# A gated cross-attention and mixture-of-experts kernel: VectorE's order in the second expert stage

## The reference, cut to what matters

```python
def _L1_ffn_ref(x, Wg, W1, b1, W2, b2, W3, b3):
    weights, indices = _gate(x2, Wg)            # 4 of 16 experts per token
    for e in range(E):
        we = jnp.sum(weights * (indices == e), axis=-1)
        h = jax.nn.silu(x2 @ W1[e].T + b1[e]) * (x2 @ W3[e].T + b3[e])
        y = y + (h @ W2[e].T + b2[e]) * we[:, None]
```

## Time and profile before

| | |
|---|---|
| median of 3 runs | 2151.57 us (2151.31 to 2154.27) |
| the profiled execution | 2151.75 us |
| its span, first to last instruction | 2150.0 us |
| PE matmul busy | 1955.2 us (91% of the span) |
| DVE busy | 1348.4 us (63%) |
| POOL busy | 1147.7 us (53%) |
| ACT busy | 917.3 us (43%) |

### The profile page before, as it was taken

One profiled execution on the slowest core, in us unless ns is written; L12 is line 12 of the kernel. 1 busy time (PEld: TensorE's weight loads), 2 busy tenths in 40 slices (PEclk: granted clock), 3 DMA queues, 4 the chain that ended last, 5 costly groups with the idle time before them and its releaser, 6 DMA issues. The chain is left out here.

```text
span 2150.0 us, 40169 instructions
## 1 busy us (share of the span) xinstructions
PE 1955.2 (91%) x11418; PEld 1350.0 (63%) x11418; DVE 1348.4 (63%) x4050; ACT 917.3 (43%) x2321; POOL 1147.7 (53%) x1375
## 2 busy tenths in 40 slices
PE   5999999999999279999769999999999559999997
PEld 4777777777777168888635555555555425555554
DVE  3677777777776533223248888878888525555554
ACT  2434344444433323333247767766766213333332
POOL 1344444444444345454437888888888514444444
PEclk8999999999999689999979999999999579999999
DMA  6011101011116023333211111111117364555554
GB/s 167 26 39 27 39 27 39 27 39 37 29 53 229 8 40 52 53 50 55 43 33 36 54 54 55 55 50 50 55 55 228 99 189 81 82 82 82 80 84 64
DMA packets 140296, 142.25 MB, mean 66 GB/s; under 512 B 31626, under 2 KB 130674, under 8 KB 139832
## 3 DMA queue, kind: packets, MB, share of 16 engines
q1 hardware_dynamic: 94282, 86.60, 13.9%
q0 software_dynamic: 37888, 44.51, 12.9%
q10 hardware_dynamic: 7918, 8.57, 1.2%
HBM read 89.88 MB, written 51.94 MB: 66 GB/s over the span
## 5 line engine op out<-in xcount | busy, mean ns | idle before, releaser
L779 POOL TENSOR_SCALAR prob<-prob,rc 100x363 f32<-100x363 f32 x256 | 157.1, 623 | 355.3 <-DVE rc L634 355.3
L1826 POOL DMA_INDIRECT out<-y,xr x115 | 177.9, 1547 | 246.9 <-DVE y L1857 131.6
L1924 PE MATMUL psG<-expert_w,xgT 128*128 x460 | 219.6, 600 | 2.7 <-ACT xgT L1885 2.7
L980 PE MATMUL psJ<-wkv,cTn 96*121 96x512 f32 x384 | 180.8, 609 | 0.0
L558 ACT ACTIVATE prob<-psS,nm 100x361 f32<-100x361 f32 x256 | 141.6, 561 | 53.9 <-DVE nm L629 50.6
L1525 POOL DMA_INDIRECT acc<-y,slots x57 | 90.3, 1584 | 136.5 <-DVE y L1619 129.4
L629 DVE TENSOR_REDUCE nm<-psS 100x2 f32<-100x722 f32 x128 | 115.1, 899 | 71.8 <-PE psS L457 71.6
L1432 POOL DMA_INDIRECT rows<-row,pos_of x128 | 137.8, 1077 | 35.6 <-issue 30.1
L1889 ACT ACTIVATE gate<-pre 128x256 f32<-128x256 f32 x115 | 47.9, 416 | 249.6 <-DVE pre L1842 249.6
L1941 PE MATMUL psD<-expert_w,hT 128*128 x460 | 128.9, 402 | 12.6 <-ACT hT L1895 8.1
L1596 DVE TENSOR_TENSOR hid<-psU,gate 128x512 f32<-128x512 f32 x57 | 39.4, 692 | 159.1 <-PE psU L1716 159.1
(11 more groups left out here) (307 smaller groups left out, 5100.2 us busy)
## 6 DMA issues: line engine op xcount, KB each, us to landing
xr<-rows SPq DMA_DIRECT2D x115, 136.5 KB, 2.6
expert_w<-in_L_ffn_moe_w SPq DMA_DIRECT2D x8, 1024.0 KB, 13.8
bias<-in_L_ffn_b ACTq DMA_DIRECT2D x3, 2048.0 KB, 15.9
ctx<-in_ctx SPq DMA_DIRECT2D x32, 181.5 KB
cT<-in_ctxT SPq DMA_DIRECT2D x32, 180.5 KB
cT<-in_ctxT SPq DMA_DIRECT2D x64, 90.2 KB
expert_w<-in_L_ffn_moe_w SPq DMA_DIRECT2D x8, 512.0 KB, 12.7
expert_w<-in_L_ffn_W1T SPq DMA_DIRECT2D x16, 256.0 KB
```

The lines of the kernel that those rows point to most:

```text
L779: g.tensor_scalar(prob[:, q, :], prob[:, q, :], rc[:, q:q + 1], 1.0, ALU.mult, ALU.mult).then_inc(prob_done, 1)
L980: mm = t.matmul(ph[0:rows, 0:cols], lhs, wt[:, k, :], start=k == 0, stop=k == 1)
L1826: g.indirect_dma_start(acc, bass.IndirectOffsetOnAxis(row_token[:, j % RING, :], 0), y[:, j % 4, :], None, compute_op=ALU.add).then_inc(sc ...
L1924: mm = t.matmul(psG[:, r, :], xT[:, r, k, :], w13[:, bass.ds(e, 1), k, :], start=k == 0, stop=k == 1)
```

## The change

The step `hidden` is cut in two. `biased(j, e)` is the bias addition that writes `pre`, and `hidden(j)` is the multiplication that writes `hid`. In round j, DVE now does `biased(j+1)`, then reads the expert of tile j+2, then `weighted(j-2)`, then `hidden(j+1)`. `biased(j)` also waits for the gate of tile j-2, which reads the buffer that it writes. The registers with the expert's number are kept in a list from `biased` to `weighted`, so that each number is read once. PE, ACT, POOL and SP have the same instructions in the same order.

```diff
+                def biased(j, e):
+                    v.wait_ge(g_mm, j + 1)
+                    if j >= 2:
+                        v.wait_ge(g_out, j - 1)
+                    v.tensor_tensor(pre[:, j % 2, :], psG[:, j % 2, :], bias[:, bass.ds(e, 1), 0:2, :].rearrange("p e k f -> p (e k f)"),
+                                    ALU.add).then_inc(pre_done, 1)
+
                 def hidden(j):
-                    r, e = j % 2, expert(j)
-                    v.wait_ge(g_mm, j + 1)
-                    v.tensor_tensor(pre[:, r, :], psG[:, r, :], bias[:, bass.ds(e, 1), 0:2, :].rearrange("p e k f -> p (e k f)"),
-                                    ALU.add).then_inc(pre_done, 1)
                     v.wait_ge(g_out, j + 1)
                     if j >= 2:
                         v.wait_ge(h_mm, j - 1)
-                    v.tensor_tensor(hid[:, r, :], pre[:, r, F:2 * F], gate[:, r, :], ALU.mult).then_inc(hid_done, 1)
-
-                def weighted(j):
-                    e = expert(j)
+                    v.tensor_tensor(hid[:, j % 2, :], pre[:, j % 2, F:2 * F], gate[:, j % 2, :], ALU.mult).then_inc(hid_done, 1)
+
+                def weighted(j, e):
...
+                e_of = [expert(j) for j in range(2)]
                 v.wait_ge(bias_in, 16 * 3)
+                biased(0, e_of[0])
                 hidden(0)
                 for j in range(NT):
+                    if j + 1 < NT:
+                        biased(j + 1, e_of[j + 1])
+                    if j + 2 < NT:
+                        e_of.append(expert(j + 2))
                     if j >= 2:
-                        weighted(j - 2)
+                        weighted(j - 2, e_of[j - 2])
                     if j + 1 < NT:
                         hidden(j + 1)
-                weighted(NT - 2)
-                weighted(NT - 1)
+                weighted(NT - 2, e_of[NT - 2])
+                weighted(NT - 1, e_of[NT - 1])
```

## The result

The changed kernel takes 2112.26 us in the median of 4 runs (2109.79 to 2118.66), the kernel before 2151.72 us (2151.31 to 2154.27). The ratio is 0.9821, with a 95% interval of 0.9804 to 0.9838: 39 us less. The profiled execution took 2113.48 us, its span is 2111.7 us.

What follows compares the result with a forecast made beforehand. VectorE's closed round of 3.37 us a tile was taken as the bound, against PE's 3.022. Gains of 36.9 and 2 us less 6 for row buffers make 32.9: 2151.75 - 32.9 = 2118.9, so 2119 us, range 2110 to 2132.

Steps and rivals of the forecast that it cites:

- VectorE's ring: In the last expert stage, VectorE's closed round of dependent steps and waits: 3.37 us a tile, busy for 1.90 us of it.
- PE's own pace of 3.022 us: Time per tile where PE is not held, read from five row transposes at the start of the last stage.
- The first term: Steady part of the last stage: 106 tiles at 3.022 us in place of 3.370, 36.9 us less.
- VectorE's new round: VectorE's steps per tile after the change, from one `pre` to the next possible one: 2.46 us.
- The ring of row buffers: Load of tile j+8 waits for scatter of tile j; late scatters at 15 boundaries cost 0.4 us each, 6 us.
- The end: After the last row transpose, the last `pre` and the steps behind it come sooner: 2 us less.
- the front: Start of the stage, where VectorE waits for the bias loads: nothing moves there.
- Rival B: `y` and `hid` each hold POOL's scatter once, 0.8 us on its path; boundaries cost 15 us: 2128 us, chance 0.03.
- rows 13: POOL's scatter instructions: 1542 to 1682 ns in all 115 cases, 1546 in the middle, never held for the length of `hid`.
- Rivals A: Row buffers hold PE more often as landings get slower: 18 us in place of 6, 2131 us, chance 0.14.
- C: VectorE keeps the pace with a round of 3.2 us: 18 us gained and 1 at the end, 2133 us, chance 0.05.
- D: `hid` comes too late, so PE waits with its hidden transpose in every tile: 11 us slower, 2162 us, chance 0.02.

## Why the prediction was right, and where it was off

- The bound was VectorE's ring and not PE: right, and each of three ways to shorten it gave PE's pace. But the sum of 201.2 busy and 155.5 idle us, 3.365 a tile, proves nothing, though I used it as proof: busy and idle of any engine add up to the stretch. In the changed kernel, where PE is the bound, VectorE's 199.2 busy and 136.4 idle us make 335.6 of 334.9 as well. What told was who ended the idle pieces: reads ("issue"), the gate and its own `yb`, and never PE.
- PE's own pace of 3.022 us, read from five tiles at the start, held for 106: right to the third digit. The first term of 36.9 us came as 34.8, and the missing 2.1 are the ring's waits.
- VectorE's new round: I had 2.46 us, it is 1.95. I had put 0.15 us between steps that don't depend on each other; they overlap instead. It changed nothing here, but the same error made me miss the kernel with one uncovered read.
- The ring of row buffers: the mechanism was right, the term was mis-sized, and this is the step that failed: "I take 0.4 us for each of the 15: 6 us". It is 2.1 us in all, 0.14 each. What there was to spare came out nearly as worked out: `y` ends 14.1 us after its tile's transpose, as I had it, and the load is issued 4.5 us before use in the middle (5.95 before). But I took the size of a typical boundary from two of the longer ones, 5.55 and 6.84 us; the 16 distances over 4.2 us between two scatters were 5.3 on average before. In the changed kernel the long distances between two scatters (16 of them over 4.2 us) are 4.5 to 6.2 us, 5.0 on average, 2.0 more than a round: just what there is to spare. The one of 6.84 us did not come back.
- The end: 2 us forecast, 2.5 measured.
- Forecast 2119, measured 2112.26: of the 6.6 us, 4 are the ring, 0.5 the end, and 1 the front, where kernels and runs differ by that much without cause in this stage; the profiled run lies 1.2 above the median. The result is 0.4 us below what I had for a PE that is never held (2112.7).
- Rival B, that steps of VectorE hold up the scatters in every tile, did not come. But my reading of rows 13, that this trace does not agree with the rule, was wrong. The Trainium skill ("SBUF — State Buffer", section "Who interferes with whom") says that a VectorE step with two SBUF inputs contends with a GpSimd instruction that reads SBUF. The longest scatter before, 1.68 us, is such a case, and so is the longest of the changed kernel, 1.74 us: `hid` had just started when they started.

```profile
1947.87 0.43 DVE L1847 TENSOR_TENSOR hid<-pre,gate 128x256 f32<-128x256 f32 x1 [0.48 <-ACT gate L1889]
1948.03 1.68 POOL L1826 DMA_INDIRECT out<-y,xr  x1 [0.30 <-issue]
```
```profile
2010.46 0.42 DVE L1850 TENSOR_TENSOR hid<-pre,gate 128x256 f32<-128x256 f32 x1
2010.55 1.74 POOL L1826 DMA_INDIRECT out<-y,xr  x1 [3.39 <-DVE y L1859]
```

  A `hid` that starts later within a scatter costs it nothing: 90 of them lie wholly inside one before, and these scatters took 1.54 to 1.57 us. So the price is at most 0.27 us (1.81, the longest with the extra additions, for 1.546), and few scatters pay it.
- Rivals A, C and D did not come. What the prediction left out is that removing the read would alone have been enough. I counted the reads (0.36 and 0.48) and the gate (0.48) in the ring and treated them as one edit, though 3.37 - 3.02 = 0.35 is no more than the smallest of them, so that each was enough by its own size.

Open: why 7 buffers cost 3.57 us a tile and not 3.3 with boundaries on top (40 us forecast, 56 measured in the steady part). The lower clock makes 3.6 of the 16 us that are missing, and where the trace has the landing, loads took 2.8 us on average, where I had counted 2.3; the rest was not looked into.

## What to carry to other kernels

When an engine is busy for 97% by the profile, look at the distance between starts in a stretch where nothing holds it, and compare it with the steady distance: here 3.02 and 3.37 us. Then look at the idle pieces of the suspected partner and at what ended each of them. If none was ended by the busy engine, the partner is the bound, and only the shortfall (0.35 us) has to be removed, by whichever edit is simplest, and no more. A read into registers belongs behind a step that another wait follows, and it should be done once.

A wait at the start of a stage can cost more than its length. Here TensorE stood for 4.5 us, 6.8 us at the lower clock followed from within it, and the ninth tile came 2.8 us later than the wait alone explains.

## What the runs showed of the hardware that was not expected

- Steps on VectorE that don't depend on each other start before the one ahead has ended: 0.34 us apart for additions that take 0.42, 0.27 us from `y` (0.35) to `hid`. One that waits for the other's semaphore starts 0.15 us after its end. The Trainium skill ("VectorE: DVE Perf Modes", section "Two Vector instructions with no wait between them") gives a model for this: an instruction is held until all earlier ones have finished if an input or its output starts in another group of 32 partitions than the last one in that memory. All steps of this stage cover all 128 partitions, so they start in the same group, and the traces agree.
- Reading one number into registers costs VectorE 0.57 to 0.60 us (0.30 of it the load) when it is exposed, more than an addition of 128x256 (0.42).
- A transfer of biases in three parts of 2 MB lands part by part, at 1738.0, 1745.0 and 1750.4 us: waiting for two of three made the first step that needs them start 4.4 us sooner.
- A scatter's instruction and a VectorE step get in each other's way, but only at certain moments. Of the 1380 scatters in the twelve traces 33 took over 1.625 us (1.546 in the middle). At the start of each of the 33, a VectorE step with two SBUF inputs, or `y`, was running and had 0.2 to 0.4 us to go. At the start of 583 others it was `pre` or `yb`, which have one input in PSUM, and none of these took over 1.614 us. That is not the whole rule: 14 scatters at whose start a `y` had 0.32 to 0.35 us to go stayed at 1.55 us. The other way round, 55 of 1380 `y` took 0.40 to 0.70 us in place of 0.35, and all 55 ran during a scatter. That the shared ports are the cause is the skill's rule and fits; no experiment here set out to test it.
